# Filler writes between the loads of the full slots, an earlier quantisation of slot 4, and one output moved at the end

## The chip, the cores and the metric

The kernel runs on one core of a Trainium2 chip. The metric is the time of one execution in microseconds of the device (us), lower is better; the time before is the median of three executions.

## What is computed

Two routed layers stand behind each other. The first sends each token to one of 4 experts by its token id, the second to one of 8 experts by the largest logit, with ternary weights and rows quantised to 8 bits (cut to what matters):

```python
def xattn(h, token_ids, Wg, Wu, Wd):            # all three are ctx
    expert = minimum(clip(token_ids, 0, 24999) // 6250, 3)
    for e in range(4):
        y = (silu(h @ Wg[e].T) * (h @ Wu[e].T)) @ Wd[e]
        out = where(expert == e, y, out)
def bitlinear(x, w):
    s = 127 / clip(max(abs(x), axis=-1), 1e-5);  xq = round(x * s) / s
    m = 1 / clip(mean(abs(w)), 1e-5);            wq = clip(round(w * m), -1, 1) / m
    return xq @ wq.T
def ffn(x, router_w, wg, wu, wd):
    idx = argmax(x @ router_w.T)
    for e in range(8):
        y = bitlinear(square(relu(bitlinear(x, wg[e]))) * bitlinear(x, wu[e]), wd[e])
        out = out + where(idx == e, y, 0)
x = x + xattn(layernorm(x), token_ids, ctx, ctx, ctx)
x = x + ffn(layernorm(x), router_w, wg, wu, wd)
```

There are 2048 rows of 512 numbers; each expert matrix is 512 x 512.

## The kernel before

The kernel writes out by hand, for each engine, the order of its instructions, and joins the engines with semaphores. Everything is unrolled.

**First layer (ticks).** The rows are sorted by token id into 19 blocks of 128 (`B1`). In tick t block t is gathered and multiplied; after it each row is normalised again, the router picks one of 8 experts, and POOL scatters the finished row of 520 numbers (512 values and the factors `RSTD`, `INV`, `SCALE`, `NEG`, `TOKEN`, `CUBE`) into the scratch tensor `x1_rows` in HBM, in the region of its expert. Beside this the 24 weight matrices are loaded and made ternary.

**Second layer (slots).** 23 slots (`B2`, numbered 0 to 22) of 128 rows each go through gate, up and down products. Slots 0 to 4 (`EARLY` = 5) hold blocks that were already full after block 14. Slots 5 to 8 (up to `FULL` = 9) hold blocks that are full once all rows are stored, so they need no filler. Slots 9 to 22 can hold blocks that are only partly full: behind the last row of each of the 8 experts a block of 128 filler rows has to be written to `x1_rows` first (`fill(e)`, 260 KB each), and load 9 waits for all eight (`filled`). The names `load(s)` and `fill(e)` are those of SP's program, which issues every one of these transfers: it reads an address from SBUF into a register (TENSOR_LOAD), then issues the DMA. So fills and loads form one queue in program order. Before the change it is: fill 0 and 1; waits for the table of the slots (`slots_ready`), for the stores of the last three blocks (`row_out`) and for `y_ready`; load 5, 6, 7, 8; fill 2 to 7; wait for `filled`; load 9 to 22.

**What a slot does.** The steps of slot b, with the engine, and the line of the profile:

- DVE `quantise(b)` (L1176) turns the loaded rows into 8-bit steps (`t8`); it waits for `x1_in[b]`, which is the landing of load b.
- PE `transpose_q(b)` (L1506), ACT `evict_tT(b)` (L708), PE `gate_product(b)` and `up_product(b)` (L1512, four matmuls each).
- ACT `relu_square(b)` (L716, L720), DVE `product_of(b)` (L1186), `largest_product(b)` (L1196), `product_scale(b)` (L1204, L1207), ACT `quantise_prod(b)` (L740).
- PE `transpose_r(b)` (L1506), ACT `evict_rT(b)` (L728), PE `down_product(b)` (L1512).
- POOL `output_scale(b)` (L578), DVE `output(b)` (L1215), POOL `scatter(b)` (L583), which stores the rows to the output.

PE goes through slot u as: gate u, up u, transpose_q u+1, transpose_r u-2, down u-3. DVE's loop over u from 2 to 27 is: quantise u+1, largest_product u-1, product_scale u-1, output u-4, product_of u, with the steps of `late` (the table of slots 5 to 22) strewn between them.

**Factors in groups.** POOL computes three small tables from the loaded rows not for one slot but for a group: `GROUPS` is {0,1,2}, {3,4}, {5,6,7,8}, {9,10}, {11..14}, {15..18}, {19..22}. `factors_of(group)` waits for every load of its group, then writes `cap_scale` (L570), `down_size` (L571) and `least_max` (L573). It stands in POOL's order at u = first slot of the group less one, behind `scatter(u - 4)`. `product_scale(b)` on DVE waits for the tables of its group:

```python
for s in slots:                                   # factors_of, POOL
    pool.wait_ge(x1_in[s], 16)
dve.wait_ge(sizes, SIZES * (group_of(b) + 1))     # product_scale, DVE
```

Of the kernel before, what the change touches and what calls it, by code (L numbers as in the profile page):

```python
# [21 lines left out]
E1, E2 = 4, 8  # L22
B1 = TILES + E1 - 1
B2 = TILES + E2 - 1
# [20 lines left out]
EARLY, EARLY_AFTER = 5, 14  # L45


FULL = 9
# [24 lines left out]
ORDER = [m for m in range(MATS) if m not in EXTRA]  # L73
ABOVE = 2
assert len(ORDER) == TICKS + ABOVE
FIRST_FILLS = 2
X_MATRIX = 19
X_USERS = range(RING - 1, B1, RING)
SUM_PIECES = 4
# [10 lines left out]
def moe_program(nc, x_in, tokens_in, ctx_in, router_in, weights_in, out):  # L90
    with ExitStack() as whole:
# [145 lines left out]
        def staged_of(i):  # L237
            return staged_early[i - 2] if i in (2, 3) else staged[i % 2][:, :]
# [6 lines left out]
        def cols_of(slots, col, n=1):  # L245

            if slots[0] < EARLY:
                tile, first = staged[slots[0] // 3], slots[0] % 3
            else:
                tile, first = late_rows, slots[0] - EARLY  # L250
            if len(slots) == 1:
                return tile[:, first * ROW + col:first * ROW + col + n]
            three = tile[:, first * ROW:(first + len(slots)) * ROW].rearrange("p (s c) -> p s c", c=ROW)
            return three[:, :, col:col + n]
# [79 lines left out]
        @block.sync  # L334
        def _(sp):
            sp.dma_start(token_ids[:, :], tokens_in).then_inc(token_in, 16)
            sp.dma_start(router[:, :], router_in).then_inc(router_landed, 16)
            def load_context(e):
                sp.dma_start(ctx_raw[e], ctx_in[e]).then_inc(ctx_in_sem[e], 16)

            def load_weights(i):
                if i in (2, 3):
                    sp.dma_start(staged_of(i), weights_in[ORDER[i]]).then_inc(staged_early_in[i - 2], 16)
                    return
                if i >= 4:

                    last = i - 4 if i < 6 else i - 2
                    sp.wait_ge(dve_part, last + 1)
                    sp.wait_ge(act_part, last + 1)
                sp.dma_start(staged_of(i), weights_in[ORDER[i]]).then_inc(staged_in[i % 2], 16)  # L350

            load_context(0)
            load_weights(0)
            load_context(1)
            load_weights(1)

            sp.wait_ge(gathering, 2)
            load_context(2)
            load_weights(2)
            load_weights(3)  # L360
            load_context(3)
            for i in range(4, len(ORDER)):
                load_weights(i)
                if i == 5:
                    sp.wait_ge(made, 12)
                    sp.dma_start(x1_rows[FILLER_BLOCK:SCRATCH_ROWS], filler[:, :]).then_inc(filler_out, 16)
                if i == FIRST_PIECE[0] + ABOVE + 1:
                    sp.wait_ge(ctx_lo_ready, E1)
                    sp.dma_start(extra, weights_in[EXTRA[0]]).then_inc(extra_in, 16)
                if i == FIRST_PIECE[1] + ABOVE + 1:  # L370
                    sp.wait_ge(extra_part, SCALE_PIECES)
                    sp.dma_start(extra, weights_in[EXTRA[1]]).then_inc(extra_in, 16)

            def load(s):
                first = sp.value_load(base[s >= EARLY][s:s + 1, 0:1], min_val=0, max_val=SCRATCH_ROWS - P)  # L375
                sp.dma_start(cols_of([s], 0, ROW), x1_rows[bass.ds(first, P)]).then_inc(x1_in[s], 16)  # L376


            sp.wait_ge(slots_ready, 1)
            for b in range(EARLY_AFTER - ROWS + 1, EARLY_AFTER + 1):  # L380
                sp.wait_ge(row_out[b % ROWS], landed(b))
            for s in range(EARLY):
                if s % 3 == 0:
                    sp.wait_ge(dve_part, len(ORDER) - 1 + s // 3)
                    sp.wait_ge(act_part, len(ORDER) - 1 + s // 3)
                load(s)


            def fill(e):
                last = sp.value_load(bound[0:1, e:e + 1], min_val=0, max_val=FILLER_BLOCK - P)  # L390
                sp.dma_start(x1_rows[bass.ds(last, P)], filler[:, :]).then_inc(filled, 16)  # L391

            sp.wait_ge(bound_ready, 1)
            for e in range(FIRST_FILLS):
                fill(e)
            sp.wait_ge(slots_ready, 2)
            for b in range(B1 - ROWS, B1):
                sp.wait_ge(row_out[b % ROWS], landed(b))
            sp.wait_ge(y_ready, B1)
            for s in range(EARLY, FULL):  # L400
                load(s)
            for e in range(FIRST_FILLS, E2):
                fill(e)
            sp.wait_ge(filled, E2 * 16)
            sp.wait_ge(filler_out, 16)
            for s in range(FULL, B2):
                load(s)
# [390 lines left out]
        def _(dve):  # L798
# [390 lines left out]
            def largest_product(b):  # L1189
                if not 0 <= b < B2:  # L1190
                    return
                dve.wait_ge(prod_ready, b + 1)
                if b >= 2:
                    dve.wait_ge(out_scale_ready, b - 1)
                f = fac[b % 2]
                dve.tensor_reduce(f[:, 0:1], prod[b % 2][:, :], X, ALU.max,  # L1196
                                  apply_absolute_value=True).then_inc(amax_ready, 1)

            def product_scale(b):
                if not 0 <= b < B2:  # L1200
                    return
                f = fac[b % 2]
                dve.wait_ge(amax_ready, b + 1)
                dve.reciprocal(f[:, 1:2], f[:, 0:1]).then_inc(inv_ready, 1)  # L1204
                dve.wait_ge(sizes, SIZES * (group_of(b) + 1))
                dve.wait_ge(inv_ready, b + 1)
                dve.tensor_scalar(f[:, 2:3], f[:, 1:2], cap_scale[:, b:b + 1], QMAX, ALU.min, ALU.mult)\  # L1207
                    .then_inc(r_scale_ready, 1)

            def output(b):  # L1210
                if not 0 <= b < B2:
                    return
                dve.wait_ge(d_ready, b + 1)
                dve.wait_ge(out_scale_ready, b + 1)
                dve.scalar_tensor_tensor(cols_of([b], 0, D), down_bank(b)[:, :], out_scale[:, b:b + 1],  # L1215
                                         cols_of([b], 0, D), ALU.mult, ALU.add).then_inc(out_ready, 1)
# [128 lines left out]
            for u in range(2, STEPS):  # L1345
                next(late, None)
                next(late, None)
                if u > 2:
                    quantise(u + 1)
                next(late, None)  # L1350
                next(late, None)
                largest_product(u - 1)
                next(late, None)
                product_scale(u - 1)
                next(late, None)
                next(late, None)
                output(u - 4)
                product_of(u)

        @block.tensor  # L1360
        def _(pe):
# [210 lines left out]
            def transpose_r(b):  # L1572
                if not 0 <= b < B2:
                    return
                pe.wait_ge(r8_ready, b + 1)
                if b >= 1:
                    pe.wait_ge(rT_ready, b)
                else:
                    pe.wait_ge(choice_ready, B1)
                transpose2(rT_ps, r8).then_inc(rT_ps_ready, 1)  # L1580

            def down_product(b):
                if not 0 <= b < B2:
                    return
                pe.wait_ge(rT_ready, b + 1)
                if b == 0:
                    pe.wait_ge(cut_ready, MATS)
                    pe.wait_ge(p_ready, B1 - 1)
                elif b == 1:
                    pe.wait_ge(by_slot_ready, 2)  # L1590
                elif b < B2 - 2:
                    pe.wait_ge(out_ready, b - 1)
                elif b == B2 - 2:
                    pe.wait_ge(prod_ready, B2 - 1)
                else:
                    pe.wait_ge(relu_ready, B2 - 1)
                product2(down_bank(b), rT[b % 2], ffn_expert[b], 2).then_inc(d_ready, 1)
# [61 lines left out]
            for u in range(3, B2):  # L1659
                gate_product(u)  # L1660
                up_product(u)
                load_ffn_expert(u + 1)
                transpose_q(u + 1)
                if u == 3:
                    spread_means(1)
                transpose_r(u - 2)
                down_product(u - 3)
            transpose_r(B2 - 2)
            down_product(B2 - 3)
            down_product(B2 - 2)  # L1670
            transpose_r(B2 - 1)
            down_product(B2 - 1)
# [28 lines left out]
```

## Time and profile before

| | |
|---|---|
| median of three executions | 262.27 us (261.54 to 262.48) |
| the profiled execution: its own time | 262.27 us |
| its span, first to last instruction | 260.4 us, mean granted clock 0.990 |
| busy PE / DVE / ACT / POOL | 236.2 / 218.8 / 211.3 / 163.6 us |
| ticks end, slots begin | about 175 to 180 us from the start of the span |
| last output scatter issued | 255.81 us |

All moments below are in us from the start of the span. A row of a timeline has its start, the time it took (merged instructions count from the first start to the last end), the engine, the line of the kernel before, the operation, and in brackets how long the engine stood idle before it and who ended that idle time. SPq is SyncE's own queue; its DMA rows are the issue of a transfer, not the transfer.

### The profile page before, as it was taken

What the parts mean: (1) busy time and instruction counts of PE and PEld (TensorE: products, weight loads), DVE (VectorE), ACT (ScalarE), POOL (GpSimd) and SP (SyncE); (2) the same over time, 40 slices, a digit from 0 to 9 for tenths busy, and PEclk for the clock granted to TensorE, in tenths of its full rate; (3) what the DMA queues carried; (4) which work ended last, traced back from release to release, by engine and by line L of the source; (5) the groups of instructions that cost most, each with busy time, mean ns of one, the idle gap of its engine ahead of it and who ended that gap; (6) DMA issues with size and microseconds to landing.
All of it is one profiled execution on the core that took longest, in us unless ns stands there. A gap on an engine that the chain in (4) does not pass through costs nothing.

```text
span 260.4 us, 5809 instructions
## 1 busy us (share of the span) xinstructions
PE 236.2 (91%) x1410; PEld 172.6 (66%) x1420; DVE 218.8 (84%) x680; ACT 211.3 (81%) x322; POOL 163.6 (63%) x318
## 2 busy tenths in 40 slices
PE   2388999999999999999999999989899799999970
PEld 2245688888888888888888888875445355555530
DVE  5978999989889988899888798788888599999860
ACT  1865799899887988889888799688989699998950
POOL 4462565767876776767767545568646376657553
PEclk9999999999999999999999999999999999999996
DMA  6969972955755565885556543354386799211110
GB/s 214 425 209 373 401 280 99 364 168 213 242 190 184 163 181 221 309 291 156 171 208 245 202 150 139 120 166 120 117 259 253 240 285 292 85 38 69 63 40 0
DMA packets 13839, 51.72 MB, mean 199 GB/s; under 512 B 2862, under 2 KB 2862, under 8 KB 10224
## 3 DMA queue, kind: packets, MB, share of 16 engines
q1 hardware_dynamic: 8928, 37.91, 41.9%
q0 software_dynamic: 4880, 13.44, 14.7%
q8 instruction: 14, 0.23, 0.4%
q14 instruction: 17, 0.14, 0.1%
HBM read 40.49 MB, written 13.48 MB: 207 GB/s over the span
## 4 chain that ended last, share of the span: by engine, by line
PE 77%; DVE 6%; issue 4%; SPq 4%; DMA 4%; ACT 2%; POOL 1%; POOLq 0%; DVEq 0%; ACTq 0%
PE bank L1404 39%; PE bank L1512 15%; PE bank L1390 10%; PE bank L1484 6%; PE bank L1506 3%; PE bank L1601 2%; PE bank L1423 1%; SPq L390 1%; DMA late_rows<-x_rows 1%; DMA x_rows<-filler 1%; SPq L391 1%; SPq L375 1%; DMA x_rows<-row,store_at 1%; POOL out_rows L583 1%; SPq L376 1%
## 5 line engine op out<-in xcount | busy, mean ns | idle before, releaser
L1512 PE MATMUL bank<-ternary,qT 128*128 x179 | 43.4, 379 | 0.5 <-issue 0.2
L628 ACT ACTIVATE ternary<-staged 128x2048 bf16<-128x2048 f32 x20 | 38.0, 1898 | 1.1 <-DMA staged<-weight_chunks 1.1
L634 ACT ACTIVATE ternary<-staged,w_scale 128x1536 int16<-128x1536 f32 x20 | 31.5, 1576 | 2.2 <-DVE w_scale L909 0.6
L531 POOL DMA_INDIRECT x_rows<-row,store_at x19 | 22.5, 1183 | 14.5 <-POOL store_at L523 10.3
L1512 PEld LDWEIGHTS bank<-ternary,qT 128*128 128x128 bf16 x184 | 17.7, 97 | 20.7 <-issue 5.2
L583 POOL DMA_INDIRECT out_rows<-late_rows x18 | 19.7, 1095 | 16.7 <-DVE late_rows L1215 14.8
L681 ACT ACTIVATE p<-bank,rstd 128x512 f32<-128x512 f32 x19 | 13.0, 686 | 14.6 <-PE bank L1404 14.6
L465 POOL DMA_INDIRECT x<-x_rows,gather x16 | 19.1, 1193 | 9.2 <-issue 5.4
L1512 PE MATMUL bank<-ternary,rT 128*128 x87 | 22.6, 379 | 1.0 <-ACT rT L728 0.8
L989 DVE SCALAR_TENSOR_TENSOR p<-bank,rstd,p 128x512 f32<-128x512 f32 x19 | 14.2, 749 | 10.0 <-ACT p L681 10.0
L1404 PE MATMUL bank<-ctx_hi,pT_hi 128*128 x76 | 22.4, 416 | 0.3 <-DVE pT_lo L998 0.3
L1404 PE MATMUL bank<-ctx_hi,hT_hi 128*128 x76 | 22.3, 414 | 0.0
L1404 PE MATMUL bank<-ctx_lo,hT_hi 128*128 x76 | 20.4, 391 | 0.2 <-DVE ctx_lo L895 0.2
L1484 PEld LDWEIGHTS bank<-router,x1T 128*128 128x128 f32 x152 | 19.7, 191 | 1.4
L1404 PE MATMUL bank<-ctx_lo,pT_hi 128*128 x76 | 20.5, 392 | 0.0
L1404 PE MATMUL bank<-ctx_hi,pT_lo 128*128 x76 | 20.4, 390 | 0.0
L1404 PE MATMUL bank<-ctx_hi,hT_lo 128*128 x76 | 20.3, 389 | 0.0
L1484 PE MATMUL bank<-router,x1T 128*128 128x8 f32 x152 | 18.2, 246 | 0.0
L716 ACT ACTIVATE relu<-bank 128x512 f32<-128x512 f32 x23 | 13.7, 596 | 4.2 <-PE bank L1512 4.2
L708 ACT ACTIVATE qT<-bank 128x512 bf16<-128x512 int16 x23 | 13.5, 586 | 4.3 <-PE bank L1506 4.2
L503 POOL TENSOR_TENSOR row<-ln,half_powers 128x2 f32<-128x2 f32 x19 | 13.8, 727 | 4.9 <-DVE squares L1024 4.9
L1186 DVE TENSOR_TENSOR prod<-bank,relu 128x512 f32<-128x512 f32 x23 | 15.8, 686 | 1.3 <-ACT relu L720 0.5
(222 smaller groups left out, 663.2 us busy)
## 6 DMA issues: line engine op xcount, KB each, us to landing
staged<-weight_chunks SPq DMA_DIRECT2D x20, 1024.0 KB, 5.3
late_rows<-x_rows SPq DMA_DIRECT2D x18, 260.0 KB, 3.5
ternary<-ctx_chunks SPq DMA_DIRECT2D x4, 1024.0 KB, 5.8
ternary<-weight_chunks SPq DMA_DIRECT2D x4, 1024.0 KB, 10.0
x_rows<-filler SPq DMA_DIRECT2D x9, 260.0 KB
staged<-x_rows SPq DMA_DIRECT2D x5, 260.0 KB, 2.9
x_rows<-row,store_at POOLq DMA_INDIRECT x19, 5.7
out_rows<-late_rows POOLq DMA_INDIRECT x18
```

Source lines behind the costliest of these rows:

```text
L465: pool.indirect_dma_start(x[b % RING], None, x_in, bass.IndirectOffsetOnAxis(ap=gather1[:, b:b + 1], axis=0), bounds_check=N - 1, oob_is_e ...
L503: pool.tensor_tensor(r[:, RSTD:INV + 1], s[:, 2:4], half_powers[:, :], ALU.pow).then_inc(norm2, 1)
L531: pool.indirect_dma_start(x1_rows, bass.IndirectOffsetOnAxis(ap=store_at[b % ROWS][:, :], axis=0), row[b % ROWS][:, :], None, bounds_check ...
L583: pool.indirect_dma_start(out, bass.IndirectOffsetOnAxis(ap=cols_of([b], TOKEN).bitcast(I32), axis=0), cols_of([b], 0, D), None, bounds_ch ...
L628: nc.scalar.activation(ternary[:, m * K * D:(m + 1) * K * D], staged_of(i), ACT.Abs, accum_out=abs_sum[:, 2 * i:2 * i + 1]).then_inc(abs_r ...
L634: nc.scalar.activation(ternary[:, m * K * D + DVE_COLS:(m + 1) * K * D].bitcast(I16), staged_of(i)[:, DVE_COLS:], ACT.Copy, scale=w_scale[ ...
L989: dve.scalar_tensor_tensor(p[:, :], a_ps[b % 2][:, :], rstd1[b % 2][:, :], p[:, :], ALU.mult, ALU.mult).then_inc(p_ready, 1)
L1186: dve.tensor_tensor(prod[b % 2][:, :], u_ps[b % 2][:, :], relu2[:, :], ALU.mult)\
L1390: last = pe.transpose(ps[:, k * P:(k + 1) * P], src[:, k * P:(k + 1) * P], ident[:, :])
L1404: last = pe.matmul(ps[:, :], left[:, k * P:(k + 1) * P], right[:, bass.ds(e * (K * D) + k * D, D)], start=(n == 0 and k == 0), stop=(n == ...
L1484: last = pe.matmul(logits_ps[:, 0:E2], x1T[:, k * P:(k + 1) * P], router[:, k * E2:(k + 1) * E2], start=(k == 0), stop=(k == K - 1))
L1512: last = pe.matmul(ps[:, :], left[:, k * P:(k + 1) * P], ternary[:, bass.ds(e * (3 * K * D) + (kind * K + k) * D, D)], start=(k == 0), sto ...
```

## The change

Three edits, none of which adds or removes work. The constant `FIRST_FILLS` goes, so lines behind it move up by one at first.

- SP: fills 0 to 3 stand ahead of the waits in place of fills 0 and 1; behind load 5 and 6 come fills 4 and 5, behind load 7 fills 6 and 7, then load 8, and then the wait for `filled` as before.
- DVE: `quantise(4)` moves from u = 3 to u = 2, ahead of `largest_product(1)`; at u = 23 `output(19)` moves ahead of `product_scale(22)`.
- PE: `down_product(20)` moves ahead of `transpose_r(21)`.

```diff
             sp.wait_ge(bound_ready, 1)
-            for e in range(FIRST_FILLS):
+            for e in range(E2 // 2):
                 fill(e)
             sp.wait_ge(slots_ready, 2)
...
             sp.wait_ge(y_ready, B1)
-            for s in range(EARLY, FULL):
+            load(EARLY)
+            load(EARLY + 1)
+            for e in range(E2 // 2, E2 - 2):
+                fill(e)
+            load(EARLY + 2)
+            for e in range(E2 - 2, E2):
+                fill(e)
+            for s in range(EARLY + 3, FULL):
                 load(s)
-            for e in range(FIRST_FILLS, E2):
-                fill(e)
             sp.wait_ge(filled, E2 * 16)
...
-                if u > 2:
+                if u > 3:
                     quantise(u + 1)
                 next(late, None)
                 next(late, None)
+                if u == 2:
+
+                    quantise(4)
                 largest_product(u - 1)
                 next(late, None)
+                if u == B2:
+
+                    output(u - 4)
                 product_scale(u - 1)
                 next(late, None)
                 next(late, None)
-                output(u - 4)
+                if u != B2:
+                    output(u - 4)
                 product_of(u)
...
+            down_product(B2 - 3)
             transpose_r(B2 - 2)
-            down_product(B2 - 3)
             down_product(B2 - 2)
```

SP's queue before: load 8, then the last fill and the start of load 9 (`base1` holds the addresses of slots 5 to 22, `bound` those of the fillers; each pair of TENSOR_LOAD and DMA is one load or one fill):

```order
L375 TENSOR_LOAD base1
L375 ISA x2
L376 ISA
L376 DMA late_rows<-x1_rows 128x520
...
L390 TENSOR_LOAD bound
L390 ISA x2
L391 ISA
L391 DMA x1_rows<-filler 128x520
L375 TENSOR_LOAD base1 [waits filler_out,filled]
```

and after the change the last fill, load 8 and the start of load 9:

```order
L389 TENSOR_LOAD bound
L389 ISA x2
L390 ISA
L390 DMA x1_rows<-filler 128x520
L374 TENSOR_LOAD base1
L374 ISA x2
L375 ISA
L375 DMA late_rows<-x1_rows 128x520
L374 TENSOR_LOAD base1 [waits filler_out,filled]
```

Load 8 was the fourth DMA behind the waits for the stores and is now the eighth; the last fill was the last DMA ahead of the wait for `filled` and is now the one ahead of load 8.

DVE at u = 23, before (`fac0` are the scales of slot 22, `bank6`, `bank5`, `bank2` and `bank3` the down products of slots 19 to 22):

```order
L1196 TENSOR_REDUCE fac0<-prod0 128x1 [waits out_scale_ready,prod_ready]
L1204 RECIPROCAL fac0<-fac0 128x1 [waits amax_ready]
L1207 TENSOR_SCALAR fac0<-fac0,cap_scale 128x1 [waits inv_ready,sizes]
L1215 SCALAR_TENSOR_TENSOR late_rows<-bank6,out_scale,late_rows 128x512 [waits out_scale_ready,d_ready]
L1215 SCALAR_TENSOR_TENSOR late_rows<-bank5,out_scale,late_rows 128x512 [waits out_scale_ready,d_ready]
```

and now:

```order
L1200 TENSOR_REDUCE fac0<-prod0 128x1 [waits out_scale_ready,prod_ready]
L1219 SCALAR_TENSOR_TENSOR late_rows<-bank6,out_scale,late_rows 128x512 [waits out_scale_ready,d_ready]
L1208 RECIPROCAL fac0<-fac0 128x1 [waits amax_ready]
L1211 TENSOR_SCALAR fac0<-fac0,cap_scale 128x1 [waits inv_ready,sizes]
L1219 SCALAR_TENSOR_TENSOR late_rows<-bank5,out_scale,late_rows 128x512 [waits out_scale_ready,d_ready]
```

One output stands between the largest value of slot 22 and its scale.

## Rows read from the trace of the kernel before

**Rows 1.** Waits of all engines, one pair: us in total, times, longest.
```profile
DVE t L1176 <- DMA late_rows<-x_rows: 4.3, 2, 3.0
```
**Rows 2.** Timeline of PE where slots 5, 7, 8 and 9 begin.
```profile
188.36 1.89 PE L1512 MATMUL bank<-ternary,qT 128*128 x8
190.44 0.40 PE L1506 MATMUL bank<-ident,t 128*128 128x128 bf16 x4 [0.19 <-DVE t L1176]
...
191.76 1.89 PE L1512 MATMUL bank<-ternary,qT 128*128 x8
...
195.04 1.89 PE L1512 MATMUL bank<-ternary,qT 128*128 x8
...
198.08 1.89 PE L1512 MATMUL bank<-ternary,qT 128*128 x8
...
204.97 0.40 PE L1506 MATMUL bank<-ident,t 128*128 128x128 bf16 x4 [1.75 <-DVE t L1176]
...
206.29 1.89 PE L1512 MATMUL bank<-ternary,qT 128*128 x8
```
**Rows 3.** Timeline of DVE, slots 5 to 9.
```profile
189.83 0.55 DVE L1176 TENSOR_SCALAR t<-late_rows 128x512 int16<-128x512 f32 x1 [1.33 <-DMA late_rows<-x_rows]
...
197.07 0.22 DVE L1207 TENSOR_SCALAR fac<-fac,cap_scale 128x1 f32<-128x1 f32 x1
...
198.46 0.54 DVE L1176 TENSOR_SCALAR t<-late_rows 128x512 int16<-128x512 f32 x1
...
204.36 0.55 DVE L1176 TENSOR_SCALAR t<-late_rows 128x512 int16<-128x512 f32 x1 [3.00 <-DMA late_rows<-x_rows]
```
**Rows 4.** SP's queue, each timeline row a window around one issue.
```profile
184.42 0.35 SPq L391 DMA_DIRECT2D x_rows<-filler  x1
...
187.13 0.36 SPq L376 DMA_DIRECT2D late_rows<-x_rows  x1
189.37 0.34 SPq L376 DMA_DIRECT2D late_rows<-x_rows  x1
```
**Rows 5.** Chain that ended last: start, us, what.
```profile
183.78 2.48 DMA x_rows<-row,store_at
...
197.82 2.69 DMA x_rows<-filler
...
201.56 2.78 DMA late_rows<-x_rows
```
**Rows 6.** Load issues at L376: the one issued at 189.37, then the one at 202.89.
```profile
DMA to landing us min/median/max: 3.2/3.2/3.2
...
DMA to landing us min/median/max: 4.2/4.2/4.2
```
**Rows 7.** Timeline of POOL, the tables of slots 5 to 8.
```profile
194.19 0.21 POOL L570 TENSOR_TENSOR cap_scale<-late_rows,by_slot 128x4 f32<-128x4 f32 x1
...
194.50 1.04 POOL L573 TENSOR_TENSOR least_max<-cap_scale,minus_one 128x4 f32<-128x4 f32 x1
```
**Rows 8.** Timeline of ACT, the eviction of slot 4.
```profile
187.27 0.60 ACT L708 ACTIVATE qT<-bank 128x512 bf16<-128x512 int16 x1
```
**Rows 9.** Timeline of PE, then ACT, DVE and POOL, at the end.
```profile
249.42 0.40 PE L1506 MATMUL bank<-ident,r 128*128 128x128 bf16 x4 [0.49 <-ACT r L740]
...
252.63 1.03 PE L1512 MATMUL bank<-ternary,rT 128*128 x4 [0.77 <-ACT rT L728]
...
250.35 0.71 ACT L740 ACTIVATE r<-prod,fac 128x512 int16<-128x512 f32 x1
...
250.21 2.21 DVE L1215 SCALAR_TENSOR_TENSOR late_rows<-bank,out_scale,late_rows 128x512 f32<-128x512 f32 x3
253.70 0.75 DVE L1215 SCALAR_TENSOR_TENSOR late_rows<-bank,out_scale,late_rows 128x512 f32<-128x512 f32 x1 [1.28 <-PE bank L1512]
...
251.90 1.06 POOL L583 DMA_INDIRECT out_rows<-late_rows  x1 [1.57 <-DVE late_rows L1215]
...
255.81 0.98 POOL L583 DMA_INDIRECT out_rows<-late_rows  x1 [0.30 <-issue]
```

More of the change, by code:

```diff
@@ L75 @@
 assert len(ORDER) == TICKS + ABOVE
-FIRST_FILLS = 2
 X_MATRIX = 19
```

## The prediction

> **What bounds the kernel now.** I read the waits first, then the timelines around them. In the waits DVE idles 4.3 us in all for two landings of slot rows [rows 1]; those are the stalls that the edit on SP is about. PE's timeline tells what they cost. From slot to slot the gate product starts 3.04 us later where nothing is late (195.04 to 198.08) [rows 2]. At slot 5 PE waits 0.19 us, at slot 9 it waits 1.75 us, both for DVE's quantised rows [rows 2], and DVE in turn waited 1.33 and 3.00 us for loads 5 and 9 [rows 3]. Load 9 stands behind the last fill: that is issued at 197.82 and lands 2.69 us later; load 9 is issued at 201.56, lands 2.78 us later, DVE starts at 204.36, and gate 9 at 206.29 [rows 5, 3, 2]. After that PE keeps its pitch, so a shift of gate 9 is a shift of the end. The end itself is a second place: the last products and the last four scatters of POOL.
>
> The profiled execution took 262.27 us for a span of 260.4 (1.9 us lie around it), which is also the median of the three. So I add the differences to 262.27.
>
> **SP: where each transfer goes.** An issue takes 1.12 us of the queue (187.13 to 189.37 is two) [rows 4].
> - Fills 2 and 3 now stand where SP waited for the last store, from the issue of fill 1 at 184.42 to the landing at 183.78 + 2.48 = 186.26 [rows 4, 5]. Fill 3 is issued at about 184.42 + 2.24 = 186.66. Ahead of the first load the row of before needs 187.13 - 186.26 = 0.87 us from the end of the wait; with fill 3's own 0.35 us ahead, load 5 is issued at about 187.8, that is 0.7 later.
> - Load 5 landed 2.70 us after its issue (187.13 to 189.83) [rows 4, 3]. Now it lands at 190.5. DVE is idle there anyhow, so slot 5 goes 0.7 us later: gate 5 at about 192.4 instead of 191.76 [rows 2].
> - Load 8 is the fourth DMA behind the waits before, now the eighth. Counted from fill 0, the fifth transfer of the queue was issued at 189.37 and the twelfth (the last fill) at 197.82, so seven issues took 8.45 us, 1.21 each, some of them slower than 1.12 [rows 4, 5]. Now load 5 is the fifth and load 8 the twelfth: 187.8 + 8.45 = 196.25. With every issue at 1.12 us, none slower, it would be 187.8 + 7 x 1.12 = 195.6.
> - Load 9 waits for the fill ahead of load 8: issued at 195.1, landed at 197.8 by the 2.69 us of [rows 5], load 9 issued one us later at 198.9 and landed at 201.7, where DVE wants it no sooner than 202. The stall of slot 9, as it stands in the trace, is gone.
>
> **What is late next.** Load 8 is not only slot 8's. POOL's tables for slots 5 to 8 are one group and wait for all four loads. Before they began at 194.19 and `least_max` ended at 194.50 + 1.04 = 195.54 [rows 7], 1.5 us ahead of its reader, `product_scale(5)` on DVE at 197.07 [rows 3]. Now POOL stands at that wait until load 8 lands. Landing takes 2.7 us for the first load of a train, 3.2 for the third, 4.2 for one that ran beside a scatter [rows 3, 4, 6]; POOL's scatters stand behind the blocked tables, so none runs beside load 8, and I take 3.0. Load 8 lands at 199.25. From there, step by step:
> - tables on POOL, 1.35 us (194.19 to 195.54), and 0.05 to be seen: 200.65 [rows 7];
> - DVE from `product_scale(5)` to the end of `quantise(8)`: 197.07 to 199.00, 1.93 us (output 2 and product 6 between them) [rows 3];
> - PE from the end of quantise to gate 8: 204.91 to 206.29, 1.38 us [rows 3, 2];
> - gate 8 to gate 9: 3.04 us [rows 2].
>
> Together 7.75, call it 7.8: gate 9 at 207.05 instead of 206.29, so **+0.76 us**. Quantise 9 fits in at about 204.8 behind it, load 9 is there, and POOL's backlog (a held output scale, then scatters) is worked off in its idle gaps, such as the 1.57 us of [rows 9]. The bounds: with 195.6 and 2.7 us load 8 lands at 198.3 and gate 9 is at 206.1, -0.2; with 196.25 and 4.2 us it is at 208.25, +2.0.
>
> Without the group's wait gate 9 would follow gate 5 (192.4) by four pitches of 3.04, at 204.6, that is -1.7, or -1.5 with one pitch as long as the 3.28 from gate 5 to gate 6 [rows 2]. The wait gives that back.
>
> The page on DMA of the Trainium skill (DMA: Bandwidth & Descriptors, Anatomy of one DMA) fits one transfer at about 2.0 us plus its bytes at 436 GB/s, 2.6 us for 260 KB; the first load of the train agrees (2.70), the third does not (3.2). By the page load 8 would land 0.4 us sooner and the sum would be 262.2.
>
> **DVE: quantise 4 at u = 2.** It moves ahead of `largest_product(1)`, whose scale ACT needs for `quantise_prod(1)`, and pushes it back by a quantisation, half a microsecond (0.54 [rows 3]). ACT then does the relu and square of slot 3 that much later, and the eviction of slot 4 stands right behind them: at about 187.7, against 187.27 before [rows 8]. PE's transpose of slot 4 goes sooner, but gate 4 hangs on that eviction (0.60) and begins at about 188.3, against 188.36 [rows 2]. Whatever is won there, 0.2 us at most, runs into load 5, which holds slot 5 anyhow; a loss would have up to two microseconds of DVE's idle time ahead of slot 5 to vanish in (1.33 before, plus the 0.7 of load 5) [rows 3]. I count 0.
>
> **The end.** Before, PE waits 0.49 us at 249.42 for the scale step of slot 21 and only then does down 20 [rows 9]; now down 20 fills that wait, ends about 249.7, transpose 21 follows at once, down 21 needs its eviction (0.6 us, like [rows 8]) and ends at about 251.6. On DVE output 19 begins 0.5 us sooner and is a 0.74 us step in front of the scale of slot 22, so ACT's step for slot 22 moves from 250.35 to about 250.95 and ends at 251.65; transpose 22 (0.4) and its eviction (0.6) follow, and down 22 goes from 252.63 to about 252.8 [rows 9]. Output 22 ends 0.15 later, at 254.6. But the last scatter was not held by it: four scatters run from 251.90 to 255.81 at 1.30 us each, while output 22 was through at 254.45 [rows 9]. Scatter 19 begins 0.6 us sooner, at 251.3; then scatter 22 is free at 255.2 and its rows, 0.8 us behind the end of output 22 (POOL's lag between 253.70 + 0.75 and the scatters' start is at most 1.36), at 255.4. Take **-0.4 us**; between 0 and -0.6.
>
> Sum: 262.27 + 0.76 - 0.4 = 262.6 us.
>
> **The rivals.**
> - *Even or slightly faster or slower through the group's wait* (the forecast): 262.6, with the bounds above 262.27 - 0.2 - 0.6 = 261.5 and 262.27 + 2.0 - 0.4 = 263.9. Chance 0.83.
> - *The stall just goes*: the tables of slots 5 to 8 do not bind, because load 8 lands before they are needed (about 196.5). For it: the stall of 1.75 us is the largest on PE in this part. Against it: load 8 is issued at 195.6 at the earliest. It would give 262.27 - 1.5 - 0.4 = 260.4. Chance 0.06.
> - *Slower, through the transfers themselves*: fills and loads in turn share the engines, load 8 lands like the one at 202.89, 4.2 us, and a further pause in the issue comes ahead of it. It decides from a landing of load 8 at 200.2 on (0.95 us later than I reckon), where the time passes 263.6; with 4.2 us and a pause of 0.5 us it lands at 200.95 and gives 264.3. Against it: in the row of before a fill lands in 2.69 us in the midst of six [rows 5]. Chance 0.11. The same page (Issuing engines are not separate DMA queues) says that all queues run on the same 16 engines and interleave; the 4.2 us of a load beside a scatter agrees.
> - *The edits at the end cost instead of giving*: the held scale of slot 22 makes down 22 later than scatter 19 gains, POOL's chain being no bound. Then +0.2 instead of -0.4: 263.2, inside the same verdict. In the forecast's chance.
>
> **How the numbers follow.** About 0.5% (1.3 us) is what a measurement of this kernel can tell from no change: below 260.96 is faster, above 263.58 slower. The forecast holds 0.83, nearly all of it within 0.5%: its low bound is 261.5, its high bound shares the slower case. Faster 0.07, same 0.81, slower 0.12. The range reaches from 261.3, the low bound with 0.2 us for the spread of the runs, to 263.7; outside lie the stall that just goes and the worse half of the slower case.
>
> **What would show it.** In the new profile: load 5 issued near 187.8, load 8 near 196.2; DVE idle for 2 to 3 us ahead of `product_scale(5)`, released by POOL's `least_max`, which itself began on the landing of load 8; PE idle about 2 us ahead of the transpose of slot 8 and none ahead of slot 9; gate 9 near 207.0; PE without an idle gap ahead of down 20, and the last scatter bound by output 22 and no more by the scatters ahead of it. If DVE does not wait for `least_max` the mechanism is wrong; if it does and gate 9 is off, one of load 8's issue or landing was mis-sized.

## The result, and the profile after

The changed kernel took 262.96 us (median of 7 executions, 262.51 to 263.80) beside 261.83 us for the kernel before (7 executions): a ratio of 1.0048, 95% interval 1.0028 to 1.0067. The prediction said 262.6 us, range 261.3 to 263.7, and held "same" for the likeliest. In a second comparison on another occasion (12 executions, below) the ratio was 1.0010, 0.9981 to 1.0040. By these two ratios the change does not make the kernel faster: it costs 0.1 to 0.5%, and only the first interval lies wholly above 1.

| | before | after |
|---|---|---|
| profiled execution | 262.27 us | 262.51 us |
| span | 260.4 us | 260.7 us |
| gate 9 starts | 206.29 us | 206.91 us |
| gate 22 starts | 245.95 us | 246.42 us |
| last scatter issued | 255.81 us | 256.06 us |

Lines have moved: fills are now L390, loads L375, quantise L1180, `product_scale` L1208 and L1211, outputs L1219, POOL's tables L574 to L577, scatters L587, PE's products L1523 and its transposes L1517.

First the issues of SP, each row from a window around one issue:

```profile
187.86 0.35 SPq L375 DMA_DIRECT2D late_rows<-x_rows  x1
...
194.79 0.06 SPq L390 DMA_DIRECT2D x_rows<-filler  x1
195.62 0.35 SPq L375 DMA_DIRECT2D late_rows<-x_rows  x1
198.34 0.35 SPq L375 DMA_DIRECT2D late_rows<-x_rows  x1
```

Load 5 left at 187.86 (187.13 before [rows 4]), the last fill at 194.79 (197.82 before [rows 5]), load 8 at 195.62, load 9 at 198.34 (201.56 before). So the edit did to the fills what it says: load 9 was 3.2 us sooner. POOL's timeline shows what load 8 held:

```profile
193.52 1.20 POOL L587 DMA_INDIRECT out_rows<-staged  x1 [1.45 <-DVE staged L1219]
198.60 0.19 POOL L574 TENSOR_TENSOR cap_scale<-late_rows,by_slot 128x4 f32<-128x4 f32 x1 [3.88 <-DMA late_rows<-x_rows]
...
198.90 1.04 POOL L577 TENSOR_TENSOR least_max<-cap_scale,minus_one 128x4 f32<-128x4 f32 x1
```

POOL had scattered slot 0 and stood 3.88 us until load 8 landed; before, the tables began at 194.19 with no wait [rows 7]. DVE's timeline has the next link:

```profile
190.39 0.55 DVE L1180 TENSOR_SCALAR t<-late_rows 128x512 int16<-128x512 f32 x1 [1.41 <-DMA late_rows<-x_rows]
...
197.22 0.16 DVE L1208 RECIPROCAL fac<-fac 128x1 f32<-128x1 f32 x1
199.98 0.21 DVE L1211 TENSOR_SCALAR fac<-fac,cap_scale 128x1 f32<-128x1 f32 x1 [2.60 <-POOL least_max L577]
...
201.36 0.54 DVE L1180 TENSOR_SCALAR t<-late_rows 128x512 int16<-128x512 f32 x1
...
204.19 0.54 DVE L1180 TENSOR_SCALAR t<-late_rows 128x512 int16<-128x512 f32 x1
```

A 0.2 us instruction of slot 5 waited 2.60 us for `least_max`, and behind it in DVE's order stood output 2, product 6 and quantise 8. The 3.00 us of waiting for load 9 [rows 3] is gone: quantise 9 at 204.19 waits for nothing. PE's timeline gives the price:

```profile
186.67 0.38 PE L1545 MATMUL bank<-spread,ones 128*128 128x36 f32 x2 [0.52 <-DVE spread L1104]
...
188.63 1.90 PE L1523 MATMUL bank<-ternary,qT 128*128 x8 [0.45 <-ACT qT L712]
190.99 0.40 PE L1517 MATMUL bank<-ident,t 128*128 128x128 bf16 x4 [0.46 <-DVE t L1180]
...
192.31 1.89 PE L1523 MATMUL bank<-ternary,qT 128*128 x8
...
201.96 0.40 PE L1517 MATMUL bank<-ident,t 128*128 128x128 bf16 x4 [1.57 <-DVE t L1180]
...
203.28 1.89 PE L1523 MATMUL bank<-ternary,qT 128*128 x8
205.61 0.38 PE L1517 MATMUL bank<-ident,t 128*128 128x128 bf16 x4 [0.44 <-issue]
...
206.91 1.89 PE L1523 MATMUL bank<-ternary,qT 128*128 x8
```

The gate rows of [rows 2] are those of slots 4, 5, 6, 7 and 9. The wait of 1.75 us ahead of the transpose of slot 9 [rows 2] has become one of 1.57 us ahead of the transpose of slot 8, one slot sooner; slot 5 waits 0.46 us instead of 0.19. The 0.44 us ahead of the transpose of slot 9 are put down to "issue", that is to no other engine. They are PE's own: ahead of each transpose PE reads the expert number of the next slot from SBUF into a register (`load_ffn_expert`, L1535, in its queue of weight loads, PEldq). The reads of the whole kernel (shortest, median, longest in ns), then the one from 204.0 on:

```profile
L1535 PEldq TENSOR_LOAD <-expert x23: 302/307/1096, 172.6 to 244.2; - x23
...
L1535 PEldq TENSOR_LOAD <-expert x1: 1096/1096/1096, 204.0 to 204.0; - x1
```

This one took 1.10 us instead of 0.31. It ended at about 205.1, the register steps behind it ran to about 205.4, and the transpose began at 205.61.

At the end (PE, then ACT, DVE and POOL of the timeline):

```profile
246.42 1.89 PE L1523 MATMUL bank<-ternary,qT 128*128 x8
...
251.40 1.03 PE L1523 MATMUL bank<-ternary,rT 128*128 x4 [0.77 <-ACT rT L732]
252.27 0.39 PE L1517 MATMUL bank<-ident,r 128*128 128x128 bf16 x4
253.43 1.03 PE L1523 MATMUL bank<-ternary,rT 128*128 x4 [0.77 <-ACT rT L732]
...
251.33 0.72 ACT L744 ACTIVATE r<-prod,fac 128x512 int16<-128x512 f32 x1
...
254.50 0.75 DVE L1219 SCALAR_TENSOR_TENSOR late_rows<-bank,out_scale,late_rows 128x512 f32<-128x512 f32 x1 [1.28 <-issue]
...
251.85 1.06 POOL L587 DMA_INDIRECT out_rows<-late_rows  x1 [1.05 <-DVE late_rows L1219]
...
256.06 0.97 POOL L587 DMA_INDIRECT out_rows<-late_rows  x1 [0.59 <-issue]
```

Counted from gate 22, scatter 19 comes at 5.43 us (5.95 before) and the last scatter at 9.64 (9.86 before [rows 9]), so 0.22 us is won here. Down 21 now waits 0.77 us for its eviction, which no work covers; down 22 starts at 7.01 behind gate 22 instead of 6.68.

### The profile page after: what moved, and what is told of

It reads as the page before. It is cut to its first block, busy times and chain, and to the rows that moved or that the text cites. A ratio compares the mean times of both kernels' runs of the same rounds, so it can differ in the third digit from the quotient of the medians.

```text
span 260.7 us, 5819 instructions
## 1 busy us (share of the span) xinstructions
PE 236.9 (91%) x1420; PEld 172.9 (66%) x1420; DVE 218.6 (84%) x680; ACT 211.3 (81%) x322; POOL 163.8 (63%) x318
## 4 chain that ended last, share of the span: by engine, by line
PE 74%; DMA 6%; SPq 6%; DVE 5%; issue 4%; ACT 2%; POOL 1%; POOLq 0%; DVEq 0%
PE bank L1415 38%; PE bank L1523 16%; PE bank L1401 9%; PE bank L1495 5%; DMA staged<-weight_chunks 4%; PE bank L1517 3%; SPq L390 1%; SPq L374 1%; SPq L389 1%; DMA staged<-x_rows 1%; PE bank L1612 1%; PE bank L1434 1%; DMA late_rows<-x_rows 1%; SPq L375 1%; ACT ternary L632 1%
## 5 line engine op out<-in xcount | busy, mean ns | idle before, releaser
L1523 PE MATMUL bank<-ternary,qT 128*128 x184 | 44.0, 379 | 0.6 <-ACT qT L712 0.5
L1523 PEld LDWEIGHTS bank<-ternary,qT 128*128 128x128 bf16 x184 | 17.7, 97 | 21.3 <-issue 6.2
L587 POOL DMA_INDIRECT out_rows<-late_rows x18 | 19.6, 1090 | 17.0 <-DVE late_rows L1219 14.8
L1523 PE MATMUL bank<-ternary,rT 128*128 x92 | 23.6, 379 | 1.5 <-ACT rT L732 1.5
L744 ACT ACTIVATE r<-prod,fac 128x512 int16<-128x512 f32 x23 | 16.6, 722 | 2.6 <-DVE fac L1211 2.5
L1415 PEld LDWEIGHTS bank<-ctx_lo,hT_hi 128*128 128x128 f32 x76 | 14.2, 188 | 3.6 <-issue 0.6
```

The source lines that it names most:

```text
L587: pool.indirect_dma_start(out, bass.IndirectOffsetOnAxis(ap=cols_of([b], TOKEN).bitcast(I32), axis=0), cols_of([b], 0, D), None, bounds_ch ...
L744: nc.scalar.activation(r8[:, :], prod[b % 2][:, :], ACT.Copy, scale=fac[b % 2][:, 2:3])\
L1415: last = pe.matmul(ps[:, :], left[:, k * P:(k + 1) * P], right[:, bass.ds(e * (K * D) + k * D, D)], start=(n == 0 and k == 0), stop=(n == ...
L1523: last = pe.matmul(ps[:, :], left[:, k * P:(k + 1) * P], ternary[:, bass.ds(e * (3 * K * D) + (kind * K + k) * D, D)], start=(k == 0), sto ...
```

## The experiments

All ratios are to the kernel before, run in turn with each kernel: in the first comparison 7 executions of each, for the other kernels 8 to 12, beside 31 to 35 of before in each of three series (medians of before 262.76, 262.48 and 262.74 us). The last columns are from the profiled execution of each: gate 9 counted from gate 3, last scatter counted from gate 22. The row of gate 3 begins with its second matmul in every trace but that of the change (x7, 1.67 us long; there x8, 1.90 us, from 184.03), because the record of the first is missing; for the change too I count from the second, 184.25.

| kernel | median us | ratio (95%) | gate 3 to 9 | gate 22 to last scatter |
|---|---|---|---|---|
| before | | 1 | 22.02 | 9.86 |
| the change | 262.96 | 1.0048 (1.0028 to 1.0067) | 22.66 | 9.64 |
| the change again | 262.79 | 1.0010 (0.9981 to 1.0040) | 22.46 | 9.64 |
| SP's edit alone | 263.13 | 1.0026 (1.0008 to 1.0045) | 22.58 | 9.87 |
| quantise 4 alone | 262.09 | 0.9990 (0.9960 to 1.0019) | 21.35 | 9.87 |
| both edits at the end alone | 261.65 | 0.9966 (0.9940 to 0.9992) | 20.92 | 9.64 |
| DVE's edit at the end alone | 262.02 | 0.9966 (0.9937 to 0.9995) | 22.11 | 9.48 |
| group split alone | 262.62 | 1.0007 (0.9979 to 1.0034) | 21.91 | 9.86 |
| the change, group split | 260.51 | 0.9932 (0.9911 to 0.9953) | 20.54 | 9.64 |
| the same, quantise 4 put back | 260.71 | 0.9932 (0.9909 to 0.9955) | 20.50 | 9.64 |
| four fills, loads 5 to 8, four fills | 261.20 | 0.9957 (0.9935 to 0.9979) | 20.46 | 9.86 |
| the same, both edits at the end | 261.05 | 0.9951 (0.9927 to 0.9975) | 21.00 | 9.64 |
| the same, DVE's edit at the end alone | 260.75 | 0.9940 (0.9908 to 0.9972) | 20.64 | 9.48 |
| three fills, loads 5 to 8, five fills, DVE's edit | 261.46 | 0.9944 (0.9917 to 0.9972) | 20.56 | 9.49 |

**The three parts by themselves.** Each of these kernels has one part of the diff and leaves the rest as before. SP's edit alone:

> Only the order of fills and loads on SP is changed. Theory (the group's wait takes the place of the wait for load 9): DVE idles 2.3 to 2.9 us ahead of product_scale(5), released by POOL's least_max, PE idles 1.5 to 2 us ahead of the transpose of slot 8, gate 9 starts at 206.9 to 207.1 instead of 206.29, and the time is 0.6 to 1.1 us above the kernel before. Rival (the edit on SP is harmless, quantise 4 or the end costs): within 0.3 us of the kernel before.

DVE idled 2.62 us for `least_max`, PE 1.54 us ahead of the transpose of slot 8 and 0.90 us ahead of that of slot 5, and gate 9 started at 207.08. The time came out 0.7 us (0.2 to 1.2) above before: SP's edit carries the loss. The low end of the interval reaches the rival's 0.3 us; it is the waits in the trace that decide against it. Both edits at the end:

> Only the end is changed: output 19 ahead of the scale of slot 22, down 20 ahead of transpose 21. Theory: the last scatter starts 9.64 us behind gate 22 instead of 9.86, so 0.2 us less than the kernel before (0.4 in the prediction). Rival (the held scale of slot 22 costs more than scatter 19 gains): 0.2 us or more above the kernel before.

The last scatter came 9.64 us behind gate 22, as in the whole change. The time fell by 0.9 us (0.2 to 1.6), more than the 0.22 us of the trace, and the interval just reaches it. Part of the surplus can be seen in the profiled execution (whether the others were like it is not known): the wait of slot 9, which the edit does not touch, was 0.63 us and not 1.75 (PE's timeline of this kernel):

```profile
204.00 0.40 PE L1509 MATMUL bank<-ident,t 128*128 128x128 bf16 x4 [0.63 <-DVE t L1176]
```

Quantise 4:

> Only quantise 4 is moved. Theory: gate 4 starts within 0.3 us of 188.36 and slot 5 waits for load 5 as before, so the time is within 0.2 us of the kernel before. Rival (the delay of the scale of slot 1 goes on through ACT and is not absorbed): 0.3 to 0.5 us above it.

```profile
186.74 0.38 PE L1536 MATMUL bank<-spread,ones 128*128 128x36 f32 x2 [0.53 <-DVE spread L1100]
...
188.70 1.90 PE L1514 MATMUL bank<-ternary,qT 128*128 x8 [0.45 <-ACT qT L708]
```

and, in DVE's timeline, quantise 4 itself, longer than the 0.54 us of the others:

```profile
184.13 0.91 DVE L1176 TENSOR_SCALAR t<-staged 128x512 int16<-128x512 f32 x1
```

PE's wait for the rows of slot 4 (0.89 us before) turned into 0.53 us for DVE's `spread`, pushed back in DVE's order together with the scale of slot 1, and 0.45 us for the eviction. The second is what gate 4 starts on. Gate 4 came 4.38 us behind gate 3 instead of 4.09, gate 5 7.46 instead of 7.49: lost and absorbed, as the interval (0.9960 to 1.0019) allows.

**The whole again.**

> The changed kernel once more, beside the others of this call, since the part with only SP's edit stood 0.7 us above the kernel before and the other two parts 0.9 and 0.3 us under it, which do not add up to the +1.1 us of the whole. If the parts add, the ratio to the kernel before is 0.997 to 1.001; if they interact, it is 1.003 to 1.007 again.

It was 1.0010, which the parts add up to within their intervals (1.0026, 0.9966 and 0.9990 give 0.998). The first comparison's 1.0048 lies above the second's interval (up to 1.0040), though the two intervals overlap. The two medians stand 1.1 and 0.3 us above their own kernels before. The changed kernel came out alike in both (262.96 and 262.79 us); it is the kernel before that was lower in the first comparison, 261.83 us against 262.48 to 262.76 in the three later series. Why was not found.

**Is it the group?** The same SP order, with one line of `GROUPS` changed:

```diff
-GROUPS = [range(0, 3), range(3, EARLY), range(EARLY, FULL), range(9, 11), ...
+GROUPS = [range(0, 3), range(3, EARLY), range(EARLY, EARLY + 2), range(EARLY + 2, FULL), range(9, 11), ...
```

> The changed kernel with the group of slots 5 to 8 split in {5, 6} and {7, 8}, so that the tables of slot 5 no longer wait for load 8; POOL does 1.3 us more of table work. Theory: no idle time of DVE for least_max, none of PE ahead of slots 8 and 9, gate 9 at 204.6 to 205.2, and the time is 1.5 to 2.0 us under the changed kernel, about 1 us under the kernel before. Rival (the loads themselves are too late between the fills, the group only hides that): DVE waits for load 7 or 8 instead, gate 9 not before 206.5, time within 0.5 us of the changed kernel.

PE's timeline of this kernel, from slot 5 on:

```profile
190.69 0.40 PE L1517 MATMUL bank<-ident,t 128*128 128x128 bf16 x4 [0.60 <-DVE t L1180]
...
201.34 1.89 PE L1523 MATMUL bank<-ternary,qT 128*128 x7
...
204.38 1.89 PE L1523 MATMUL bank<-ternary,qT 128*128 x8
```

and the two tables in POOL's:

```profile
194.74 0.72 POOL L577 TENSOR_TENSOR least_max<-cap_scale,minus_one 128x2 f32<-128x2 f32 x1
...
200.36 0.74 POOL L577 TENSOR_TENSOR least_max<-cap_scale,minus_one 128x2 f32<-128x2 f32 x1
```

No wait for `least_max` and none for loads 6 to 9 was left; gate 9 came 20.54 us behind gate 3 instead of 22.66, at 204.38 and so a little sooner than expected, with the loads still between the fills. The time is 0.68% under before (1.8 us), and by the ratios 2 to 3 us under the change, somewhat more than the 1.5 to 2.0 expected. The rival, that the loads were too late by themselves, is out: the same order of loads and fills, without the shared wait, is faster than before. The split gains nothing where nothing waits for the group:

> The kernel before with the group of slots 5 to 8 split in {5, 6} and {7, 8}. Theory (before the change that group did not hold anything): within 0.3 us of the kernel before, PE's waits as there. Rival (the split has a gain of its own, by which after_split is faster): over 0.5 us under it.

1.0007, with the wait for slot 9 at 1.66 us as before. And with quantise 4 back in its old place:

> The changed kernel with the group split and quantise 4 back at its old place. Theory (moving quantise 4 only trades PE's wait for the quantised rows of slot 4 for a wait for the eviction, and load 5 holds slot 5 anyhow): within 0.3 us of after_split, ratio to the kernel before 0.991 to 0.995, gate 4 within 0.3 us. Rival (quantise 4 sooner is what lets load 5's delay be absorbed, or costs): 0.4 us or more off after_split.

0.9932 again; gate 5 came 8.10 us behind gate 3 against 8.17. With the rest in place too, moving quantise 4 is worth nothing that can be seen.

**Or the order?** The group of four is left whole, and load 8 stays with the other loads:

```diff
             sp.wait_ge(bound_ready, 1)
-            for e in range(FIRST_FILLS):
+            for e in range(4):
                 fill(e)
...
             for s in range(EARLY, FULL):
                 load(s)
-            for e in range(FIRST_FILLS, E2):
+            for e in range(4, E2):
                 fill(e)
```

> Only SP's order, in another way: fills 0 to 3 ahead of the waits as in the change, then loads 5 to 8 together, then fills 4 to 7; the group of slots 5 to 8 is as before. Theory (load 8's place in the queue holds the tables): load 8 issued near 191.2, POOL's tables before 195.5, no idle time of DVE for least_max, gate 9 at 204.6 to 205.3, and 0.5 to 1.3 us under the kernel before. Rival (load 9 is the bound again, since the last fill is no sooner): DVE waits over 1 us for load 9 and the time is that of the kernel before within 0.3 us.

Load 8 was issued at 191.38, the tables ended well ahead of need (`least_max` began at 195.30 and took 1.04 us, its reader on DVE began at 197.88), and DVE waited 0.40 us for load 9, which PE did not feel:

```profile
202.56 0.55 DVE L1180 TENSOR_SCALAR t<-late_rows 128x512 int16<-128x512 f32 x1 [0.40 <-DMA late_rows<-x_rows]
```

So two more fills in SP's idle time do all that was wanted. As far as these ratios can tell, putting fills between the loads added nothing but the held group: gate 9 stands 20.46 us behind gate 3 here, 20.54 with the group split. With the edits at the end:

> The same with the two edits at the end. Theory: 0.2 to 0.9 us under four_first, the last scatter about 9.64 us behind gate 22, and with it 1.2 to 2 us under the kernel before. Rival: the edits at the end are worth nothing, same time as four_first.

It came 0.15 us under, less than expected and within both intervals; the scatter stood at 9.64 as always, and gate 9 of this execution was 0.5 us later by two pitches of 3.39 and 3.34 us from gate 5 to 7. In both of them PE's read of the expert number was long (0.69 and 0.71 us instead of 0.31).

**The end taken apart.**

> Only output 19 ahead of the scale of slot 22; PE's order at the end is the one of before. Theory (the gain is scatter 19's, and down 20 ahead of transpose 21 costs part of it, since down 21 then waits for its eviction): the last scatter 9.45 to 9.55 us behind gate 22, against 9.64 with both edits and 9.86 with none. Rival (the two edits need each other: without PE's the scale of slot 22 comes late): 9.7 or more.

It came 9.48 us behind gate 22 in this kernel:

```profile
252.30 1.06 POOL L583 DMA_INDIRECT out_rows<-late_rows  x1 [1.06 <-DVE late_rows L1215]
...
256.35 0.97 POOL L583 DMA_INDIRECT out_rows<-late_rows  x1 [0.44 <-issue]
```

So DVE's edit gives 0.38 us, and PE's beside it takes 0.16 back (PE's alone was not tried): with down 20 first, transpose 21 starts later and down 21 has nothing in front of its wait for the eviction. In 14 traces this span has three values only: 9.86 or 9.87 without DVE's edit, 9.48 or 9.49 with it, 9.64 with both.

**Better than both.**

> Fills 0 to 3 first, loads 5 to 8 together, and at the end only DVE's edit. Theory: gate 9 at 20.4 to 20.6 us behind gate 3 (22.0 before), the last scatter 9.5 us behind gate 22, 1.3 to 2.0 us under the kernel before.

> The same with three fills ahead of the waits instead of four, so that load 5 is issued when it was before. Theory (three fit in the time that SP waits for the last store): load 5 issued within 0.15 us of 3.7 us behind fill 0 (4.4 with four), gate 5 at 7.5 us behind gate 3 instead of 8.1 to 8.2, in turn up to 0.7 us of wait for load 9; gate 9 at 20.3 to 20.9 us behind gate 3, within 0.4 us of four_first_dve. Rival (the wait for load 9 is as long as before): gate 9 at 21.3 or later.

0.9940 and 0.9944, the same within their intervals; gate 9 of the first stood 20.64 us behind gate 3, just past the 20.6 expected. With three fills ahead, load 5 left 4.22 us behind fill 0, not 3.7, for in this execution SP's read of its address took 0.66 us (chain that ended last) where 0.27 is usual:

```profile
187.59 0.66 SPq L375
```

Slot 5 therefore began 7.86 us behind gate 3, not 7.5, which was missed; gate 9 at 20.56 was as expected, DVE waiting 1.11 us for load 9 and PE not at all. The lowest median of all kernels tried is that of the change with the group split, 260.51 us. The same with quantise 4 put back (0.9932), the kernels with four fills first and an edit at the end (0.9951 and 0.9940) and the one with three (0.9944) lie inside its interval, so no winner among them is shown.

## Why the prediction was right

- **Load 5, 0.7 us later:** issued at 187.86 (said 187.8), quantised at 190.39 (190.5), gate 5 at 192.31 (192.4). Right.
- **Load 8 holds the tables of slot 5:** right in every link: POOL's wait ended by load 8, DVE's 2.60 us ended by `least_max`, PE's wait ahead of slot 8, none at slot 9. The split kernel shows that it is the cause and not a companion. For the kernel without that wait the prediction had 260.4 us; the split one took 260.51.
- **Its size, +0.76 us:** gate 9 moved by 0.62. Two terms were off and offset each other. Load 8 left at 195.62, not at 196.25: I had carried over the slow issues of before, and none of them came (7.76 us for seven issues, 1.11 each). It landed 2.71 us later (I had 3.0), and POOL began at 198.60, not 199.25. The Trainium skill (DMA: Bandwidth & Descriptors, Anatomy of one DMA) gives the fit behind the prediction's 2.6 us for transfers that GpSimd issues, and these are SP's, so that the measured 2.71 is near it settles nothing. But gate 8 to gate 9 took 3.63 us and not 3.04, through the late transpose of slot 9 and PE's read of 1.10 us ahead of it. That the forecast of gate 9 is 0.14 us off is therefore luck: 0.65 us too late here, 0.59 too early there. The read explains the smaller gaps of this kind as well. With SP's edit alone the gap was 0.21 us and the read 0.86; five other traces have gaps of 0.16, 0.19, 0.21, 0.22 and 0.32 us, each behind a read of 0.69 to 0.82 us. In the second trace of the change the pitch was 3.30 us and the read 0.75. No kernel without the read was tried, and why a read is long now and then stays open.
- **Quantise 4, counted at 0:** right in sum, wrong in its working. I had gate 4 slightly sooner; it was 0.3 us later behind gate 3, in the change and in quantise 4 alone. The step that was mis-sized is "pushes it back by a quantisation, half a microsecond": in its new place quantise 4 took 0.91 us, so the scale of slot 1 came 0.8 us later (its DVE step at 185.89 instead of 185.09), ACT's step for slot 1 began at 186.14 instead of 185.34, and the eviction of slot 4, three steps behind it, at 187.91 (said 187.7, 187.27 before). Why the quantisation is longer there is not shown. Load 5 covered it.
- **The end, -0.4 us:** measured -0.22. The step that was mis-sized is "down 21 needs its eviction (0.6 us, like [rows 8]) and ends at about 251.6": from transpose 21 to down 21 it took 250.24 to 251.40 with the semaphores, down 21 was still running when the scale step of slot 22 was done (251.33 + 0.72 = 252.05), and transpose 22 had to wait for it. Down 22, said at 6.85 us behind gate 22, came at 7.01. With PE's order of before it came at 6.85 (253.72 - 246.87, DVE's edit alone), and the scatter at 9.48, the 0.38 us that I had forecast for both. The rival in which the edits at the end cost instead of giving has a grain in it: PE's half, beside DVE's, does cost 0.16 us.
- **The median, 262.6:** 262.96 and 262.79 in two comparisons. The step that was forecast is smaller than that looks: +0.3 us to the 262.27 of before, where the medians run in turn give +1.1 and +0.3. So the mechanism is shown, but the size of the step in the median is known to about 1 us only, and that 262.6 is so near has luck in it. A part of what varies is in the kernel before: its wait for slot 9 was 1.75, 0.63, 0.94, 1.72 and 1.66 us in the five traces with its order of SP (the kernel before, both edits at the end, quantise 4, DVE's edit, the split). I took 1.75 for its fixed price.

## What to carry to other kernels

When a transfer moves back in a queue, list everyone who waits for it, not only its own consumer: here a table for a group of four slots made the last load of the group due as early as the first. A wait that is taken out of one slot is worth only what the next wait in line leaves, so price that next wait from its own landing before moving anything. And count the instructions that stand behind the held one on an in-order engine: 0.2 us of work held an output, a product and a quantisation.

## What the runs showed of the hardware

- Issuing limits this stretch, not moving: SP needs 1.1 us for each 260 KB transfer with an address read from SBUF (read, then register steps, then 0.35 us of issue), and the pace changes little whether loads or fills follow each other (from 187.86 to 195.62, load 5 to load 8, seven issues take 1.11 us each in the changed kernel, while the busy share of the DMA engines goes from 0.52 to 0.85). The Trainium skill (DMA: Bandwidth & Descriptors, Issuing engines are not separate DMA queues) calls the issuing time usually small beside the transfer; here a load lands 2.5 to 3.2 us after its issue, but a train of them advances by only 1.1 us a transfer as a rule, all of it SP's own steps.
- The reads of an address (L375, L390 before) take 0.27 us as a rule, and 0.5 to 1.06 us now and then, at other places in each execution; PE's reads (L1535) take 0.31 us as a rule, and 0.5 to 1.10 now and then.
- The wait for slot 9, which ends such a train, varied by 1.1 us between five executions with the same order, and goes with the time from the issue of load 5 to that of load 9: 14.43, 13.51, 13.76, 14.52 and 14.33 us for waits of 1.75, 0.63, 0.94, 1.72 and 1.66 us. The long reads are only a part of it. In the kernel before the read ahead of load 9 took 0.58 us and a register step of fill 4 0.46 us instead of 0.03; with the group split alone the last fill landed 3.35 us after its issue, against 2.69 before.
- A scatter on POOL starts 0.8 to 0.95 us behind the end of the output that frees it (254.50 + 0.75 to 256.06 and 250.16 + 0.74 to 251.85 in the changed kernel), but only 0.3 us behind a scatter ahead of it.
